# A gated recurrence with its state kept doubled, its recurrent products in two parts, and a filling product

## The reference, cut to what matters

```python
vz, vr, vh = video @ C_z + b_z, video @ C_r + b_r, video @ C + b
xz, xr, xh = seq @ W_z, seq @ W_r, seq @ W          # for all steps at once
def step(h, xs):
    xzt, xrt, xht = xs
    z = sigmoid(xzt + h @ U_z + vz)
    r = sigmoid(xrt + h @ U_r + vr)
    hh = tanh(xht + r * h @ U + vh)
    h_new = (1.0 - z) * h + z * hh
    return (h_new, h_new)
```

## Time and profile before

| what | value |
|---|---|
| median of 3 runs | 2583.72 us (2574.14 to 2589.09) |
| profiled execution: its own time | 2577.03 us |
| profiled execution: span, mean granted clock of PE | 2575.2 us, 0.868 |
| busy share of the span | PE 87%, PEld 61%, DVE 71%, ACT 42%, POOL 12% |
| the recurrence's 128 steps | from 23.2 us to 302.0 us of the span |
| granted clock of PE in them | 0.50 from 27 us on |

### The profile page before, as it was taken

The page is one execution under the profiler, slowest core; times in us unless marked ns, Lnnn a source line. Parts: engine busy times, 40 slices in busy tenths (PEclk is TensorE's granted clock), DMA queues, the critical chain, the costliest instruction groups (busy, mean ns, idle before and its releaser), DMA issues.

```text
span 2575.2 us, 59885 instructions
## 1 busy us (share of the span) xinstructions
PE 2242.6 (87%) x24537; PEld 1564.4 (61%) x24537; DVE 1826.1 (71%) x4255; ACT 1076.7 (42%) x2825; POOL 308.3 (12%) x535
## 2 busy tenths in 40 slices
PE   6777788998878888887899999976888799999988
PEld 4555534444455545443688888854665578888855
DVE  4444489999846777776777777725887767777776
ACT  2222146566532212113555555443444345555544
POOL 1111000000002333432000000044331000000000
PEclk6555599999877878876999999978999989999999
DMA  2000000000010000002111110005552111111111
GB/s 53 2 2 2 1 1 1 1 1 1 1 45 4 2 2 3 2 2 78 49 34 38 34 38 34 22 19 113 98 97 46 57 34 38 42 38 35 38 49 30
DMA packets 76052, 76.54 MB, mean 30 GB/s; under 512 B 15769, under 2 KB 57073, under 8 KB 74193
## 3 DMA queue, kind: packets, MB, share of 16 engines
q1 hardware_dynamic: 71872, 70.21, 10.7%
q10 hardware_dynamic: 3904, 2.49, 0.4%
HBM read 60.19 MB, written 11.82 MB: 28 GB/s over the span
## 4 chain that ended last, share of the span: by engine, by line
PE 34%; DVE 11%; ACT 6%; issue 4%; DMA 3%; ACTq 1%; SPq 0%; POOL 0%; DVEq 0%; POOLq 0%
PE B L85 33%; DVE work L1981 2%; DMA work<-work 2%; ACT hr L103 2%; DVE work L107 2%; ACT L103 1%; DVE catt L2282 1%; ACT catt L103 1%; DVE work L1985 1%; ACT work L103 1%; DVE catt L2266 1%; ACT lth L103 1%; DVE work L117 1%; ACTq L2253 1%; ACT ltc L103 1%
## 5 line engine op out<-in xcount | busy, mean ns | idle before, releaser
L85 PE MATMUL B<-gr,wres 128*128 128x512 f32 x1248 | 366.4, 422 | 25.4 <-DVE work L107 13.7
L85 PEld LDWEIGHTS B<-G,lw 128*128 128x128 f32 (+1 forms) x3256 | 260.3, 177 | 70.6 <-DVE G L107 55.4
L103 ACT ACTIVATE work<-B 128x512 f32<-128x512 f32 (+5 forms) x460 | 235.4, 531 | 145.7 <-PE B L85 83.5
L85 PE MATMUL B<-G,lw 128*128 128x32 f32 (+1 forms) x3256 | 266.2, 305 | 29.4 <-DVE G L107 27.5
L85 PEld LDWEIGHTS B<-gr,wres 128*128 128x128 f32 x1248 | 234.3, 193 | 90.1 <-DVE work L107 28.8
L85 PE MATMUL B<-work 128*128 128x128 bf16 (+3 forms) x1408 | 262.5, 314 | 27.4 <-DMA work<-work 14.0
L103 ACT ACTIVATE hr<-work 128x512 fp32r<-128x512 f32 x272 | 175.7, 646 | 136.4 <-DVE work L107 82.8
L85 PEld LDWEIGHTS B<-work 128*128 128x128 bf16 (+2 forms) x1408 | 141.9, 127 | 149.3 <-issue 84.3
L103 ACT ACTIVATE lth<-B 128x96 f32<-128x96 f32 (+1 forms) x512 | 106.3, 228 | 273.0 <-PE B L85 273.0
L1981 DVE TENSOR_TENSOR work<-work 128x512 f32<-128x512 f32 x256 | 177.5, 693 | 51.8 <-ACT work L103 45.8
L1972 DVE TENSOR_TENSOR hr<-work,hr 128x512 fp32r<-128x512 f32 x272 | 188.2, 692 | 35.2 <-ACT hr L103 35.1
(11 more groups left out here) (253 smaller groups left out, 3858.1 us busy)
## 6 DMA issues: line engine op xcount, KB each, us to landing
work<-wdr SPq DMA_DIRECT2D x128, 256.0 KB, 3.1
scr<-catt SPq DMA_DIRECT2D x144, 64.0 KB, 2.0
work<-scr SPq DMA_DIRECT2D x16, 384.0 KB
work<-scr SPq DMA_DIRECT2D x16, 192.0 KB
catt<-in_L_ffn_ew SPq DMA_DIRECT2D x24, 128.0 KB, 2.3
work<-scr SPq DMA_DIRECT2D x16, 128.0 KB
out<-work SPq DMA_DIRECT2D x32, 64.0 KB, 2.2
work<-in_x ACTq DMA_DIRECT2D x2, 512.0 KB, 5.4
```

What stands on the lines that cost most here:

```text
L85: return e.matmul(out, lhsT, rhs, start=start, stop=stop, skip_group_check=True)
L103: return e.activation(out, in_, func, bias=bias, scale=scale)
```

## The change

The state is kept as H = 2h (the copy to G halves it). With tz and tr the two tanh, `grh` = (tr + 1) H as before, `gq` = (tz - 1) H, `gzh` = (tz + 1) tanh(...), and H' = gzh - gq / 2. These are four DVE operations a step, where six stood. The next step's r and z products are no longer taken from the new state but from its two parts: gq times -U/8 (the new matrices `gn`) as soon as `gq` is there, in the step before, and gzh times U/4 (`gw`, scaled so) when `gzh` is there. So the chain goes from `gzh` straight to PE, and the new state is made beside it.

Even and odd steps have banks of their own (eight banks in use), and `gru_inputs_pe` now fills four steps of one parity. In each eight steps it has eight turns, each between a step's z product and its u product: gV for r and h (256 columns); x for r; x for h; gV and x for z (128 columns each); then the same for the odd steps. The odd steps' first four turns stand inside step 0. At the end of each step `gru_warm_pe` multiplies the identity with itself in bf16 (256 columns, twice the same 128) into a part of a bank that nobody reads. POOL scales where it copied. The two transposes of h0 and their scaling move from turn 14 to turn 122, since bank 1 is now in use.

```diff
-    def gru_banks(self, q):
-        return self.bank[6 + q % 2], self.bank[4 + q % 2]
+    def gru_banks(self, t):
+        x = 4 * (t // 8 % 2) + 2 * (t % 2)
+        return self.bank[x], self.bank[x + 1]
...
+    def gru_inputs_pe(self, e, g, odd):
+        BR, BZ = self.gru_banks(8 * g + odd)
+        R, H, Z = BR[:, 0:128], BR[:, 128:256], BZ[:, 0:128]
+        xq = self.X[:, :, 8 * g + odd:8 * g + 8:2].rearrange("p b s -> p s b")
+        if g >= 2:
+            e.wait_ge(*at("gru.hh", 8 * g - 9))
+        mm(e, BR[:, 0:256].rearrange("p (g s b) -> p g s b", g=2, s=4), self.ident[:],
+           bc(self.gV[:, 1:3, :], 2, 4), True, False)
+        yield
+        mm(e, four(R), self.gw[:, 1, :], xq, False, False)
+        yield
+        mm(e, four(H), self.gw[:, 2, :], xq, False, False)
+        yield
+        mm(e, four(Z), self.ident[:], bc(self.gV[:, 0, :], 1, 4), True, False)
+        mm(e, four(Z), self.gw[:, 0, :], xq, False, False)
         yield
...
         for t in range(T):
-            e.wait_ge(*at("gru.h", t - 1))
-            mmh(e, BR, o, gw[:, 4, :], hp).then_inc(*inc("gru.r", t))
-            mmh(e, BZ, oz, gw[:, 3, :], hp).then_inc(*inc("gru.z", t))
+            e.wait_ge(*at("gru.k", t - 1))
+            mmh(e, BR, o, gw[:, 4, :], self.gzh[:]).then_inc(*inc("gru.r", t))
+            mmh(e, BZ, o, gw[:, 3, :], self.gzh[:]).then_inc(*inc("gru.z", t))
+            if t == 0:
+                for _ in self.gru_inputs_pe(e, 0, 1):
+                    pass
+            if t % 8 == 0 and t + 8 < T:
+                ahead = chain(self.gru_inputs_pe(e, g + 1, 0), self.gru_inputs_pe(e, g + 1, 1))
+            next(ahead, None)
             e.wait_ge(*at("gru.rh", t))
-            mmh(e, BR, o + 32, gw[:, 5, :], self.grh[:]).then_inc(*inc("gru.u", t))
-            next(ahead, None)
+            mmh(e, BR, o + 128, gw[:, 5, :], self.grh[:]).then_inc(*inc("gru.u", t))
+            if t + 1 < T:
+                e.wait_ge(*at("gru.q", t))
+                mmh(e, NR, o, self.gn[:, 1, :], self.gq[:])
+                mmh(e, NZ, o, self.gn[:, 0, :], self.gq[:])
+            self.gru_warm_pe(e, t)
             yield
+    def gru_warm_pe(self, e, t):
+        B = self.gru_banks(t // 8 * 8 + 9)[1]
+        mm(e, B[:, 256:512].rearrange("p (a c) -> p a c", a=2), self.identb[:], bc(self.identb[:], 1, 2), t == 0,
+           True)
...
             e.wait_ge(*at("gru.tz", t))
-            then(e, ts(e, self.gz[:], th[:, 0, :], 0.5, ALU.mult, 0.5, ALU.add), "gru.w", "z", t)
-            then(e, e.tensor_tensor(self.ga[:], self.gz[:], hp, ALU.mult), "gru.w", "zh", t)
-            e.tensor_tensor(self.ga[:], hp, self.ga[:], ALU.subtract).then_inc(*inc("gru.w", "a", t))
+            stt(e, self.gq[:], th[:, 0, :], -1.0, hp, ALU.add, ALU.mult).then_inc(*inc("gru.q", t))
             e.wait_ge(*at("gru.hh", t))
-            then(e, e.tensor_tensor(self.gzh[:], self.gz[:], self.ghh[:], ALU.mult), "gru.w", "zhh", t)
+            stt(e, self.gzh[:], th[:, 0, :], 1.0, self.ghh[:], ALU.add, ALU.mult).then_inc(*inc("gru.k", t))
             if t >= 2:
                 e.wait_ge(*at("gru.g", t - 2))
-            e.tensor_tensor(hn, self.gzh[:], self.ga[:], ALU.add).then_inc(*inc("gru.h", t))
+            e.wait_ge(*at("gru.k", t))
+            stt(e, hn, self.gq[:], -0.5, self.gzh[:], ALU.mult, ALU.add).then_inc(*inc("gru.h", t))
...
-            e.tensor_copy(self.G[:, :, t], self.gh[t % 2][:]).then_inc(*inc("gru.g", t))
+            ts(e, self.G[:, :, t], self.gh[t % 2][:], 0.5, ALU.mult).then_inc(*inc("gru.g", t))
```

More of the change, by code:

```diff
@@ L365, in lay_gru @@
         self.gh = [sb(f"gh{i}", [128, 32]) for i in range(2)]
+        self.gn = sb("gn", [128, 2, 128])
         self.gth = sb("gth", [128, 2, 32])
@@ L405, in gru_pe @@
         e.wait_ge(*at("xin.dve", 7))
-        for _ in self.gru_inputs_pe(e, 0):
+        e.wait_ge(*at("const", "identb"))
+        for _ in self.gru_inputs_pe(e, 0, 0):
             pass
         for t in range(T):
[L409 to L413, removed]
-            e.wait_ge(*at("gru.h", t - 1))
-            mmh(e, BR, o, gw[:, 4, :], hp).then_inc(*inc("gru.r", t))
-            mmh(e, BZ, oz, gw[:, 3, :], hp).then_inc(*inc("gru.z", t))
-            e.wait_ge(*at("gru.rh", t))
-            mmh(e, BR, o + 32, gw[:, 5, :], self.grh[:]).then_inc(*inc("gru.u", t))
-            next(ahead, None)
+            g = t // 8
+            BR, BZ = self.gru_banks(t)
+            o = t % 8 // 2 * 32
+            e.wait_ge(*at("gru.k", t - 1))
[7 more added lines that the diff above has]
+            next(ahead, None)
+            e.wait_ge(*at("gru.rh", t))
+            mmh(e, BR, o + 128, gw[:, 5, :], self.grh[:]).then_inc(*inc("gru.u", t))
+            if t + 1 < T:
+                NR, NZ = self.gru_banks(t + 1)
+                o = (t + 1) % 8 // 2 * 32
+                e.wait_ge(*at("gru.q", t))
+                mmh(e, NR, o, self.gn[:, 1, :], self.gq[:])
+                mmh(e, NZ, o, self.gn[:, 0, :], self.gq[:])
+            self.gru_warm_pe(e, t)
             yield
+    def gru_warm_pe(self, e, t):
+        B = self.gru_banks(t // 8 * 8 + 9)[1]
+        mm(e, B[:, 256:512].rearrange("p (a c) -> p a c", a=2), self.identb[:], bc(self.identb[:], 1, 2), t == 0,
+           True)
     def gru_act(self, e):
@@ L428, in gru_act @@
         for t in range(T):
-            BR, BZ = self.gru_banks(t // 4)
-            o, oz = (t % 4) * 64, (t % 4) * 32
+            BR, BZ = self.gru_banks(t)
+            o = t % 8 // 2 * 32
             e.wait_ge(*at("gru.r", t))
@@ L433, in gru_act @@
             e.wait_ge(*at("gru.z", t))
-            act(e, th[:, 0, :], BZ[:, oz:oz + 32], ACT.Tanh).then_inc(*inc("gru.tz", t))
+            act(e, th[:, 0, :], BZ[:, o:o + 32], ACT.Tanh).then_inc(*inc("gru.tz", t))
             e.wait_ge(*at("gru.u", t))
-            act(e, self.ghh[:], BR[:, o + 32:o + 64], ACT.Tanh).then_inc(*inc("gru.hh", t))
+            act(e, self.ghh[:], BR[:, o + 128:o + 160], ACT.Tanh).then_inc(*inc("gru.hh", t))
             yield
     def gru_dve(self, e):
-        at, inc, then, gw, gb, th = self.at, self.inc, self.then, self.gw, self.gb, self.gth
+        at, inc, gw, gb, th = self.at, self.inc, self.gw, self.gb, self.gth
         e.wait_ge(*at("ld.gates"))
-        for i in (0, 1, 3, 4, 5, 6, 7):
+        for i in (0, 1):
+            ts(e, self.gn[:, i, :], gw[:, 3 + i, :], -0.125, ALU.mult)
+        for i in (0, 1, 6, 7):
             ts(e, gw[:, i, :], gw[:, i, :], 0.5, ALU.mult)
+        for i in (3, 4, 5):
+            ts(e, gw[:, i, :], gw[:, i, :], 0.25, ALU.mult)
         ts(e, gb[:, 0:2], gb[:, 0:2], 0.5, ALU.mult).then_inc(*inc("gru.w", "w"))
+        e.memset(self.gzh[:], 0.0).then_inc(*inc("gru.k", -1))
         e.memset(self.gh[1][:], 0.0).then_inc(*inc("gru.h", -1))
@@ L525, in mprep_pe @@
     def mprep_pe(self, e):
-        for _ in range(14):
+        for _ in range(T - 6):
             yield
@@ L535, in mprep_act @@
             yield
+        e.wait_ge(*self.at("ld.mamba"))
+        act(e, self.alog[:], self.alog[:], ACT.Exp).then_inc(*self.inc("mprep.act", "A"))
+        for _ in range(T - 20):
+            yield
         e.wait_ge(*self.at("mprep.h0"))
         act(e, self.h0T[:], self.bank[1][0:64, 0:256], ACT.Copy, scale=0.5).then_inc(*self.inc("mprep.act", "h0"))
-        act(e, self.alog[:], self.alog[:], ACT.Exp).then_inc(*self.inc("mprep.act", "A"))
     def mprep_dve(self, e):
```

20 lines of the change are left out of this document (4 added, 16 removed).

## The result

The changed kernel takes 2548.93 us (median of 4 runs, 2543.63 to 2556.56), against 2579.98 us of the kernel before on the same chip (4 runs, 2574.14 to 2589.09): ratio 0.9893, 95% interval 0.9865 to 0.9922. It is faster by 31 us; 60 were forecast. The profiled execution took 2553.23 us, its span 2551.5, against the 2577.03 of before.

What follows compares the result with a forecast made beforehand. The chain around each recurrence step was taken as the bound: 127 x 1.62 = 205.7, + 5.4 + 3.2 + 1.4 + 0.9 = 216.6 against 276.9, 60 us less: 2524 us. Range of 8 in 10: 2508 to 2589.

Steps and rivals of the forecast that it cites:

- The clock decides: Recurrence: PE is granted full clock, near 1.00 from 27 until about 225 us, giving steps of 1.62, not 1.75.
- both rows: Clock comparisons: later recurrence at full clock, 32 quartered records per 2.32 us; old step 1 losing it, 24 in 1.85.
- rival 1: Recurrence: clock holds only in part, half the steps at either level; 2556 us; 0.19 together with rival 4.
- the last eight steps: Recurrence's end: the last seven steps have no input products and the clock may fall, +0.13 each, 0.9 us.
- in time: Ahead of the u product at full clock: a turn of 128 columns costs the chain nothing.
- The z turn: Ahead of the u product at full clock: its 256 columns leave PE 0.09 late; wide turns total 5.4 us.
- step 0: Recurrence's start: takes in odd steps' inputs and the next's first piece, 1,024 columns, +1.4 us.
- rival 2: Recurrence: clock stays at 1.2 GHz after the first steps; steps 2.20, +5 us, 2589; chance 0.17.
- the q products without a wait: PE behind the u product: `gq` is done at 0.30, so q products wait next to nothing.
- POOL's scaling: POOL scales instead of copying: taken as 0 on the chain, operation at most 0.53, upper bound 0.2 a step.
- rival 4: DVE waits for POOL at full clock: up to 25 us back, 2549; 0.19 together with rival 1.
- Rival 3: PE array's changes of form cost twice a step: slower, 2610 us, deciding above 2.27 at half clock; chance 0.08.

Runs made afterwards that it cites:

- all edits: The change with two fillers a step, the waits ahead of `grh` swapped, preparation in more turns, x copied into a row by ACT: 2532.3 us, ratio 0.9815.
- x in a row: The changed kernel with input products reading 128 values of x in a row instead of strided (computes other numbers): 2548.5 us, ratio 0.988 to the kernel before.
- two fillers, swapped, spread: The changed kernel with two filling products a step, the two waits ahead of `grh` swapped, and DVE's Mamba preparation cut in more turns: 2537.5 us, ratio 0.9848.
- before with fillers: The kernel before with two filling products of 256 columns behind each step's last product, nothing else changed: 2617.9 us, ratio 1.0168.
- inputs behind u: The changed kernel with the input products put behind the u product and q products, ahead of the filler: 2634.2 us, ratio 1.0215 to the kernel before.
- the spread preparation: The changed kernel with DVE's Mamba preparation cut in more turns (`wout`, `dcol`, `dg`): 2549.3 us, ratio 0.9891 to the kernel before.

## Why the prediction was wrong, step by step

**The step that failed** is the one under "The clock decides": that the change, standing above both rows, is granted the full clock, near 1.00 from 27 to about 225 us. The clock was taken as one state for all 120 steps with input products. It isn't: with one filler it was lost for 85.4 us in the profiled execution, and what came was nearest to rival 1, "the clock holds only in part": 85.4 of 242 us at half, some 40 steps where it had put half of them, and 2549 where it said 2556. That its number came so near is partly luck: it had too much half clock, and lacked two terms of 10 us and the 9 us behind the recurrence. Nor is its reason shown, a fall in a stretch of narrow steps: narrow and wide steps alternate in pairs throughout, and the clock held for 123 us of them and was at half for 41. Of the 85.4 us, 13.7 lie in the last eight steps, whose clock the sum had priced. For the other 71.7, at 2.20 us for what takes 1.75 at full clock, 71.7 x (1 - 1.75/2.20) = 15 us went there. The argument used the nearest stretch with full clock, and ranked the change above it by counting records; a count was no measure. Between 70.8 and 111.8 us PE was busy for 40.7 of 41 us and had half the clock.

**Two terms of the sum were too small**, 10.5 us together. The chain at full clock was 1.69 in narrow turns, not 1.62: 60 x 0.07 = 4.2. The step had counted ACT to `grh` at 0.23, as before, though `grh` now waits for two things; and it had called a turn of x "in time", though x is read with a stride; the row of X that it used for the filler, 0.68, gives 0.26 + 0.68 - 0.07 = 0.87, 0.06 late. The z turn was taken as 0.09 late and was 0.30 (1.92 less 1.62): 30 x 0.21 = 6.3. The turn with gV's 256 columns, 1.70, was right (1.71).

**Sum again.** Forecast 216.6 us, of them 1.4 ahead of the first `gzh`; + 15 for the clock + 10.5 = 242. Measured: 1.8 + 242.4 = 244.2. The rest lies in step 0 (0.4), in the last eight steps (14.9 us where the sum has 13.9) and in the steps of the preparation. With all edits: 218.5 + 2.4 ahead of it = 220.9, of them some 2 for the clock between 46.1 and 53.0 us, against 216.6. These edits took away just the two terms that were too small, so this kernel confirms the rest of the sum to 2 or 3 us, not the forecast for the change. In the profiled executions 60 us were forecast and 24 came: 28 were missing in the recurrence, 9 behind it.

**Right:** 2.20 us a step at half clock; rival 2's +5 (the run without filler, +4); step 0 (+1.4, measured +1.8); the q products without a wait; POOL's scaling at nothing (0.31 of the 0.53 taken as bound), so rival 4 didn't happen; the filler in its slot. Rival 3 (changes of the array's form) was to decide above 2.27 us a step at half clock; it is 2.20, and the wide turn there is as forecast to 0.02. What the form costs on the way to a wide product is in the 0.26 (140.59 to 140.86 at full clock, 0.27); on the way back no cost shows.

**Behind the recurrence** the prediction had "the stages as before, 60 us earlier". From the last `gzh` to the end it was 2273.7 us in the kernel before and 2282.7 in the changed one, 9 us that don't come from the change's code. With them goes more half clock: 426 us behind the recurrence, 400 before. Over the profiled executions of all kernels this stretch, with the same instructions, took from 2268.3 us (x in a row, 357 us of it at half clock) to 2294.9 (two fillers, swapped, spread; 418); over all 13 the longer ones are those with more half clock (correlation 0.81, some 0.3 us for each us of it). The four with a recurrence at half clock (before, no filler, before with fillers, inputs behind u) took 2276 in the mean, the last of them 2283.0; the nine others 2281, with 401 and 402 us at half clock in the mean. Whether a faster recurrence costs something later, or these 5 us are chance, stays open: one profile of each kernel can't tell. It matters for the best kernel: its recurrence ends 56.0 us earlier, its profiled execution is 46.3 faster.

**Open too:** why the clock falls at 41.6 to 46.6 us in every kernel that had it, long step or not (PE's waits for DVE beside POOL are the untested candidate, but the fall at 234.6 us had none), and what brings it back at 50 us in one execution and at 132 in another. Only the spread preparation was aimed at the first of these, and it didn't settle it.

## What to carry to other kernels

If a kernel's gain hangs on TensorE's clock, treat the clock as a share of the time, not as a yes or no, and price both levels; then look whether there is room for more filling work in slots that the chain leaves. Before a product is called "in time", look at how its operand is read: the price from a row of another operand is a price for that operand's stride. Where two things are late by the same amount, taking either away shows nothing; take both away before either is called harmless.

## What the runs showed of the hardware

- A strided x product of 128 columns (float32, two records) held PE 0.53 us at full clock and 0.32 when read in a row; at half clock both steps were 1.98 and 2.41.
- A DVE operation with two waits started 0.30 us behind its last releaser when that was the second in the program, 0.23 when it was the first.
- TensorE had half the clock over 41 us in which it was busy for 40.7 (70.8 to 111.8), and fell to half at 234.6 us after 120 us without a wait over 0.21.
- One filling product cost no step anything where PE had room (2.41 and 1.98 with and without it); the second cost 0.14 a step at half clock and nothing at full. One or none of it decided between full clock for 157 us and for 3.5 of the recurrence.
- DVE's operations next to POOL's selection of 1.14 us took 0.77 for 0.19 (`gzh`) and 1.38 for 0.48 (`dg`).
